# Turning finished tiles into columns by transposing transfers on SP's queue, in a two-layer transformer kernel

## Chip, cores and metric

The kernel runs on one core of one Trainium2 chip. The metric is the device time of one execution in microseconds; lower is better. The kernel before takes 1585.8 us (median of 3 runs).

## The reference

Four sequences of 512 tokens with 512 features go through two layers, each an attention part and a feed-forward part; after each of the four parts the residual is added and the sum is normalised over its 512 features (layer norm without weights). All weights are dense float32 except those of the first feed-forward part, which are int8 with a scale per column.

```
x = LN(x + lightning_attention(x))      # 16 heads of 32, rotated q and k, causal with decay, chunks of 128, then w_proj
x = LN(x + ((silu(x @ Wg * sg) * (x @ Wu * su)) @ Wd) * sd)                # 512 -> 2048 -> 512
x = LN(x + (x@Wq+bq) * cumsum((x@Wk+bk) * (x@Wv+bv), over tokens) * sigmoid(x@Wgt+bgt))
x = LN(x + mixture_of_experts(x))       # 32 experts of 192, top 8 of a softmax, the 5th to 8th choice rerouted by similarity
```

## The kernel before

Tokens are handled in NT = 16 tiles of P = 128, four tiles (TB) to a sequence. `X` holds the tiles by rows, one token per partition, in float32. A matrix product needs the tokens as columns, features on the partitions, so `XT` holds every tile a second time, transposed, as two float16 halves (a high half and the remainder) of four 128 x 128 blocks each. The kernel synchronises by hand: each engine has its own instruction stream, in the order of the code, and waits on semaphores.

A finished tile (number n, counted over all stages: 0 to 15 from attention, 16 to 31 from the feed-forward part, 32 to 47 from gated attention) gets into `XT` in these steps. VectorE (DVE) or ScalarE (ACT) writes the normalised tile to `X` and raises `x_new`. ACT copies it to float16, the high half of a small buffer (`hlA` in attention, the two places of `hlB` in the feed-forward part, the four places `hl4` in gated attention), and raises `x_hi`. GpSimd (POOL) subtracts to get the low half (`x_low`, line 1686) and raises `x_lo`. TensorE (PE) makes eight transposes of 128 x 128 float16 into one PSUM bank (`xt_transposes`, line 545), raising `xt_trans`, and ACT copies the bank to `XT` (`xt_copy`, line 1400), raising `xt_new` by one. All copies of ACT are put down to line 1395 in the profile.

Attention (0 to 318 us) is a loop over the 16 tiles. In step t, PE transposes q and k of tile t (line 602), makes the output projection of tile t-1 (line 652), the state update (line 636), scores (lines 616 and 617), the products with the state (line 627), the q and k projections of tile t+1 (line 562), the eight transposes of tile t-1 (line 551), the products with the chunk (line 644) and the v projection of tile t+1 (line 562). SyncE (SP) issues four transfers per step, `swap(t)` (line 394), that exchange the partition halves of q; they wait for the two copies out of PSUM (`evac_act`, `evac_dve`), and the scores wait for them. The transposes of tile 15 come in round 7 of the first feed-forward group.

The feed-forward part (318 to 666 us) has four groups of four tiles, each of 16 rounds m. A round is 8 gate matmuls (line 706), 8 up matmuls (line 712) and 8 down matmuls of the round before (line 735). ACT does silu of the gate (line 1508), the float16 half of the product, and a copy for weight preparation; DVE the rest. The gate matmuls of a round wait for the silu of the round before. The norms of the group before are made in rounds 0 to 4; in rounds 5 to 8 of groups 1 to 3 ACT fills `hlB` for one tile each, and PE transposes these in rounds 7 to 10. Beside this, in every round, the experts' weights are split into two halves for later: SP stores 640 KB to HBM (line 432) and loads the next 640 KB (line 428), four rounds ahead.

Gated attention (666 to 885 us) has four rounds q, one per sequence, each of four steps of 48 matmuls (line 562; `gate_proj`). ACT and POOL normalise and split the four tiles finished before; in round q these are tiles 28 to 31 for q = 0, then 32 to 35 and so on. PE transposes them in steps 1 and 2 (`norm_transposes`), and after step 2 of rounds 1 to 3 makes the router's `logits` for the sequence finished before from `XT` (line 562, 48 matmuls of 32 columns). The four tiles of the last sequence follow after the rounds. SP stores the halves by rows and `X` to HBM (`store_rows`, lines 497 and 498), waiting for `x_lo` of each tile.

After that come the routing tables (to 957 us), 159 blocks of experts (to 1541 us) and the last norm.

Of the kernel before, what the change touches and what calls it, by code (L numbers as in the profile page):

```python
# [24 lines left out]
P = 128  # L25
# [12 lines left out]
EPS = 1e-5  # L38
NBLK = TOK * TOPK // P + EXPERTS - 1
# [44 lines left out]
def build(nc, ins, out):  # L84
    ctx = ExitStack()
    with ctx:
# [287 lines left out]
        def _(sp):  # L374
# [24 lines left out]

            swap(0)  # L400
# [6 lines left out]
            load_piece(12)  # L407
            swap(2)
            load_piece(13)
            load_x(2)  # L410
            swap(3)
            load_piece(14)
            load_x(3)
            swap(4)
            load_piece(15)
            swap(5)
            swap(6)
# [5 lines left out]
            with sp.Fori(7, NT) as t:  # L423
                swap(t)
# [14 lines left out]
            prep_load(1, 2)  # L439
            sp.wait_ge(state_lo, NT + 1)  # L440
# [6 lines left out]
            for m in range(NM):  # L447
                sp.wait_ge(wp_lo, m + 1)
                prep_store(m // 2, m)
                prep_load((m + 4) // 2, m + 4)  # L450
                if m % 2 == 0 and m // 2 + 1 < len(wc_pieces):
                    sp.wait_ge(wc_lo, m // 2 + 1)
                    sp.dma_start(wcraw, wc_pieces[m // 2 + 1][0]).then_inc(wc_raw, 16)
            with sp.Fori(1, BATCH - 1) as g:
                for m in range(NM):
                    sp.wait_ge(wp_lo, g * NM + (m + 1))
                    prep_store(g * 8 + m // 2, m)
                    prep_load(g * 8 + (m + 4) // 2, m + 4)
            for m in range(NM):
                sp.wait_ge(wp_lo, (BATCH - 1) * NM + m + 1)  # L460
                prep_store((BATCH - 1) * 8 + m // 2, m)
                if m + 4 < NM:
                    prep_load((BATCH - 1) * 8 + (m + 4) // 2, m + 4)

# [38 lines left out]

            for b in range(BATCH - 2):
                store_rows(b)
                store_weights(b)
# [49 lines left out]
        def _(pe):  # L556
# [98 lines left out]
            def attention(t, first, last):  # L655
# [42 lines left out]
            def ffn(g, first):  # L698
                for m in range(NM):
                    s = g * NM + m  # L700
                    if m == 0:
                        pe.wait_ge(xt_new, g * TB + TB)
# [14 lines left out]
                    if first and m == 7:  # L717
                        xt_transposes(pe, NT - 1, NT - 1, hlA, bank[3])
# [49 lines left out]
            def norm_transposes(q, tt):  # L768
                n = 2 * NT - TB + q * TB + tt
                pe.wait_ge(xt_new, n)  # L770
                xt_transposes(pe, n, None, hl4[tt], bank[3])

            def logits(b):
# [5 lines left out]
                pe.wait_ge(xt_new, 2 * NT + (b + 1) * TB)  # L779
# [41 lines left out]
            for s in range(BATCH * KD):  # L821
                q, et = s // KD, s % KD
                if et == 0:
                    pe.wait_ge(xt_new, NT + (q + 1) * TB)
# [13 lines left out]
                if et == 2:  # L838
                    norm_transposes(q, 3)
# [3 lines left out]
                if et == 1:  # L843
                    norm_transposes(q, 0)
# [5 lines left out]
            for tt in range(TB):  # L850
                norm_transposes(BATCH, tt)
# [536 lines left out]
        def _(act):  # L1388
# [11 lines left out]
            def xt_copy(n, t, src):  # L1400
                act.wait_ge(xt_trans, n + 1)
# [51 lines left out]
            def attention(t, first, last):  # L1453
# [32 lines left out]
                if not first:  # L1486
                    xt_copy(t - 1, t - 1, bank[5])
# [15 lines left out]
            def ffn(g, first):  # L1503
                n0 = g * TB + (NT - TB)
                for m in range(NM):
# [14 lines left out]
                    if first and m == 1:  # L1520
                        act.wait_ge(x_new, NT)
                        act.wait_ge(xt_trans, NT - 1)
                        copy(hlA[:, 0, :], tile(NT - 1)).then_inc(x_hi, 1)
                    if first and m == 7:
                        xt_copy(NT - 1, NT - 1, bank[3])
# [6 lines left out]
                    if not first and 7 <= m < 7 + TB:  # L1532
                        xt_copy(n0 + (m - 7), n0 + (m - 7 - NT), bank[3])
# [7 lines left out]
            def high_half(q, tt):  # L1541
# [4 lines left out]
                act.wait_ge(xt_trans, 2 * NT - TB if q == 0 else n - TB + 1)  # L1546
# [22 lines left out]
            def norm_copy(q, tt):  # L1569
                n = 2 * NT - TB + q * TB + tt  # L1570
                xt_copy(n, n % NT, bank[3])
# [14 lines left out]
            for s in range(BATCH * KD):  # L1586
                q, et = s // KD, s % KD
                if et == 2:
                    norm_copy(q, 0)
# [13 lines left out]
                if et == 2:  # L1603
                    norm_copy(q, 1)
                    if q >= 2:
                        row_hots(q - 2, 0, 8)
                    norm_copy(q, 2)
# [3 lines left out]
                if et == 2:  # L1611
                    norm_copy(q, 3)
# [10 lines left out]
            for tt in range(TB):  # L1623
                norm_copy(BATCH, tt)
# [308 lines left out]
```

## Time and profile before

| | |
|---|---|
| median of 3 runs | 1585.8 us (1585.67 to 1586.67) |
| profiled execution | 1585.89 us, span 1584.0 us |
| PE busy | 1448.3 us (91% of the span) |
| DVE, ACT, POOL busy | 952.9, 732.3, 776.5 us |
| mean granted TensorE clock | 0.961 of full speed |
| transfers issued from SP | 183.08 MB, 35.0% of 16 DMA engines over the span |

The profile is taken from one execution; its span runs from the first to the last instruction, and the execution's own time is 1.9 us longer. Busy times of engines overlap. The profile also shows the chain of work that ended last, followed back from the last instruction to what released each step.

### The profile page before, as it was taken

To read this page: it belongs to the slowest core of one execution; us is meant where nothing else is said; L and a number is where in the kernel's file an instruction comes from. 1 tells how busy PE (TensorE), PEld (TensorE's weight loads), DVE (VectorE), ACT (ScalarE), POOL (GpSimd) and SP (SyncE) were. 2 spreads that over 40 slices of the span, in tenths; PEclk is the share of its full clock that TensorE was granted. 3 is DMA by queue.
4 is the path that set the end of the run, shared out by engine and by line. 5 is a ranking of instruction groups with operands and counts; after the bars stand their busy time and mean duration, and the time that the engine had idled before them with its cause. 6 is when DMAs were issued, how large, how long until landed. Compare 5 with 4: busy or idle time off the path is not lost.

```text
span 1584.0 us, 33491 instructions
## 1 busy us (share of the span) xinstructions
PE 1448.3 (91%) x11191; PEld 820.2 (52%) x11192; DVE 952.9 (60%) x1858; ACT 732.3 (46%) x1326; POOL 776.5 (49%) x691
## 2 busy tenths in 40 slices
PE   5999999999999999999998358999999999999990
PEld 2566666544444444445454215666666666666650
DVE  7877777776757666634988883444444444444435
ACT  6544433555464645444446442444444444444443
POOL 3565544530010202044445536777777777777655
PEclk9999999999999999999999668999999999999995
DMA  6323111269776868531101444888989898876767
GB/s 242 107 81 107 27 40 26 77 219 315 238 255 232 265 222 268 179 139 54 55 3 54 158 165 93 185 183 166 202 177 206 177 196 186 162 108 96 177 76 230
DMA packets 102991, 243.45 MB, mean 154 GB/s; under 512 B 21481, under 2 KB 23049, under 8 KB 101904
## 3 DMA queue, kind: packets, MB, share of 16 engines
q1 hardware_dynamic: 67312, 183.08, 35.0%
q0 software_dynamic: 35616, 59.58, 23.0%
q8 instruction: 34, 0.56, 0.1%
q14 instruction: 29, 0.24, 0.0%
HBM read 158.92 MB, written 101.71 MB: 165 GB/s over the span
## 4 chain that ended last, share of the span: by engine, by line
PE 68%; DVE 16%; issue 6%; POOL 4%; ACT 3%; DMA 2%; SPq 0%; DVEq 0%; POOLq 0%; ACTq 0%
PE bank L894 20%; PE bank L915 11%; PE bank L562 8%; PE bank L706 6%; PE bank L712 6%; PE bank L735 6%; PE bank L885 5%; PE bank L904 2%; ACT ARENA L1395 1%; POOL ARENA L1695 1%; DVE ARENA L1032 1%; POOL ARENA L1690 1%; DVE ARENA L1266 1%; DVE ARENA L985 1%; PE bank L551 1%
## 5 line engine op out<-in xcount | busy, mean ns | idle before, releaser
L894 PE MATMUL bank<-ARENA,XT 128*128 x1908 | 364.2, 327 | 2.2 <-issue 1.1
L1826 POOL DMA_INDIRECT accs<-X,WA x159 | 252.5, 1588 | 98.8 <-issue 34.7
L894 PEld LDWEIGHTS bank<-ARENA,XT 128*128 128x128 f16 x1908 | 180.4, 98 | 124.2 <-issue 8.2
L1356 DVE COPY XT<-bank 128x1024 f16<-128x1024 f16 x159 | 109.9, 691 | 182.3 <-PE bank L885 181.1
L1819 POOL DMA_INDIRECT XT<-x_rows,WA x159 | 166.5, 1047 | 87.0 <-issue 39.8
L1395 ACT ACTIVATE ARENA<-ARENA 128x512 f16<-128x512 f32 (+2 forms) x128 | 89.3, 709 | 245.5 <-DVE ARENA L1114 134.1
L915 PE MATMUL bank<-ARENA,XT 128*128 x795 | 197.4, 379 | 0.9 <-issue 0.9
L1649 ACT ACTIVATE XT<-bank 128x192 f32<-128x192 f32 x159 | 52.5, 330 | 287.7 <-PE bank L894 287.7
L562 PE MATMUL bank<-XT,STG 128*128 128x512 f16 x640 | 151.8, 385 | 4.6 <-DVE ARENA L1160 4.3
L1677 POOL TENSOR_TENSOR rstd<-mv,mhalf 128x1 f32<-128x1 f32 x28 | 8.7, 309 | 258.2 <-DVE mv L964 258.2
L1395 ACT ACTIVATE XT<-bank 128x384 f16<-128x384 f16 (+2 forms) x207 | 125.7, 607 | 9.5 <-PE bank L551 9.0
L562 PE MATMUL bank<-WA,XT 128*128 128x512 f16 (+1 forms) x732 | 127.1, 327 | 2.4 <-DVE ARENA L1013 1.6
L735 PE MATMUL bank<-ARENA 128*128 128x512 f16 x512 | 121.0, 379 | 3.5 <-DVE ARENA L1120 3.4
L706 PE MATMUL bank<-XT,WA 128*128 (+1 forms) x512 | 122.6, 383 | 1.0 <-issue 1.0
L1366 DVE SCALAR_TENSOR_TENSOR XT<-bank,XT 128x192 f32<-128x192 f32 x159 | 66.4, 418 | 95.0 <-ACT XT L1649 91.8
L712 PE MATMUL bank<-XT,ARENA 128*128 (+1 forms) x512 | 121.7, 381 | 0.0
L1686 POOL TENSOR_TENSOR ARENA<-X,ARENA 128x512 f16<-128x512 f32 (+1 forms) x48 | 66.6, 1401 | 88.5 <-ACT ARENA L1395 88.5
L885 PE MATMUL bank<-ident,XT 128*128 128x128 f16 x1272 | 97.8, 220 | 5.5 <-DMA XT<-x_rows,WA 5.5
L915 PEld LDWEIGHTS bank<-ARENA,XT 128*128 128x128 f16 x795 | 71.7, 98 | 57.3 <-issue 1.4
L562 PEld LDWEIGHTS bank<-XT,STG 128*128 128x128 f16 x640 | 62.1, 99 | 74.8 <-DVE ARENA L1160 5.6
L885 PEld LDWEIGHTS bank<-ident,XT 128*128 128x128 f16 x1272 | 85.0, 98 | 25.7 <-issue 6.0
L1395 ACT ACTIVATE X<-bank 128x512 f32<-128x512 f32 x159 | 93.1, 586 | 2.1 <-PE bank L915 2.1
(245 smaller groups left out, 2369.6 us busy)
## 6 DMA issues: line engine op xcount, KB each, us to landing
w_scratch<-WA SPq DMA_DIRECT2D x64, 640.0 KB, 3.9
ARENA<-w_scratch SPq DMA_DIRECT2D x64, 640.0 KB
ARENA<-w_exp SPq DMA_DIRECT2D x48, 640.0 KB, 5.2
WA<-w_exp SPq DMA_DIRECT2D x16, 640.0 KB, 5.1
ARENA<-ARENA SPq DMA_DIRECT2D x64, 128.0 KB, 2.3
accs<-ARENA SPq DMA_DIRECT2D x20, 256.0 KB, 3.1
X<-x SPq DMA_DIRECT2D x4, 1024.0 KB, 6.6
ARENA<-wc SPq DMA_DIRECT2D x8, 512.0 KB, 6.0
```

The source lines that it names most:

```text
L562: mm = pe.matmul(dst, wa(a, k), wb(b, k), start=n == 0, stop=n == 3 * KD - 1)
L706: mm = pe.matmul(bank[0][:, :], Wg[:, n % KD, m * P:(m + 1) * P], XT[:, n // KD, n % KD, tk], start=n == 0, stop=n == 2 * KD - 1)
L712: mm = pe.matmul(bank[1 + m % 2][:, :], Wu[:, n % KD, m * P:(m + 1) * P], XT[:, n // KD, n % KD, tk], start=n == 0, stop=n == 2 * KD - 1)
L735: mm = pe.matmul(bank[4 + tt][:, :], fB[:, m % 2, a, tt * P:(tt + 1) * P], Wd[:, m, :], start=m == 0 and a == 0, stop=m == NM - 1 and a == 1)
L885: mm = pe.transpose(d[:, c * P:(c + 1) * P], xg[k.u % NG].bitcast(F16)[:, c * P:(c + 1) * P], ident16[:, :])
L894: mm = pe.matmul(d, xTb[k.u % 2][:, a * KD + kd, :], weights(sl, b, kd * 2 * DFF, 2 * DFF), start=(a, b, kd) == (0, 0, 0), stop=(a, b, kd) ...
L915: mm = pe.matmul(d, hT[k.u % 2][:, c, :], weights(sl, j, c0, DIM), start=n == 0, stop=n == 4)
L1356: dve.tensor_copy(xTb[k.u % 2].rearrange("p c n -> p (c n)"), bank[k.u % 2][:, :].bitcast(F16)).then_inc(xt_sb, 1)
L1395: return act.activation(dst, src, ACT.Copy, scale=scale)
L1686: pool.tensor_tensor(hl[:, 1, :], tile(t), hl[:, 0, :], ALU.subtract).then_inc(x_lo, 1)
L1819: pool.indirect_dma_start(xg[i % NG], None, xrows, bass.IndirectOffsetOnAxis(blkidx[:, i:i + 1], 0), bounds_check=TOK - 1, oob_is_err=Fals ...
L1826: pool.indirect_dma_start(accs, bass.IndirectOffsetOnAxis(blkout[:, i:i + 1], 0), yD[i % 8], None, compute_op=ALU.add).then_inc(y_out[i % ...
```

## The change

The 44 tiles 0 to 43 get into `XT` by one transposing transfer each, SBUF to SBUF, that SP issues. PE's transposes and ACT's copies of these tiles are gone; tiles 44 to 47, the last sequence, keep them. `xt_new` now rises by 16 with each landed transfer, and all waits on it are scaled; `MOVED` is 3 * 16 - 4 = 44.

```diff
+MOVED = 3 * NT - TB
...
+            def xt_move(n, t, hl):
+                sp.wait_ge(x_lo, n + 1)
+                if isinstance(n, int):
+                    sp.wait_ge(xt_new, n * 16)
+                sp.dma_start_transpose(XT[:, :, :, bass.ds(t * P, P)].rearrange("p a k n -> p (a k) n"),
+                                       hl.rearrange("p a n -> p (a n)")).then_inc(xt_new, 16)
```

SP's order. In attention the transfer of tile t-2 stands ahead of `swap(t)`; that of tile 14 behind the first loads of expert weights; that of tile 15 in round 3 of the first feed-forward group. In groups 1 to 3 they stand in rounds 5 to 8, behind the round's store and load. In gated attention the four of a round stand ahead of `store_rows`.

```diff
             with sp.Fori(7, NT) as t:
+                xt_move(t - 2, t - 2, hlA)
                 swap(t)
...
             prep_load(1, 2)
+            xt_move(NT - 2, NT - 2, hlA)
             sp.wait_ge(state_lo, NT + 1)
...
+                if m == 3:
+                    xt_move(NT - 1, NT - 1, hlA)
             with sp.Fori(1, BATCH - 1) as g:
                 for m in range(NM):
                     sp.wait_ge(wp_lo, g * NM + (m + 1))
                     prep_store(g * 8 + m // 2, m)
                     prep_load(g * 8 + (m + 4) // 2, m + 4)
+                    if 5 <= m < 5 + TB:
+                        xt_move(g * TB + (NT - TB + m - 5), g * TB + (m - 5 - TB), hlB[:, m % 2])
...
             def store_rows(b):
+                if b < BATCH - 1:
+                    for tt in range(TB):
+                        xt_move(2 * NT + b * TB + tt, b * TB + tt, hl4[tt])
...
+            for tt in range(TB):
+                xt_move(2 * NT - TB + tt, NT - TB + tt, hl4[tt])
             for b in range(BATCH - 2):
                 store_rows(b)
```

PE, in attention, the feed-forward part and gated attention:

```diff
-                if not first:
-                    pe.wait_ge(s_decayed, t * 4 + 4)
-                    xt_transposes(pe, t - 1, t - 1, hlA, bank[5])
...
-                        pe.wait_ge(xt_new, g * TB + TB)
+                        pe.wait_ge(xt_new, g * (16 * TB) + 16 * TB)
...
-                    if first and m == 7:
-                        xt_transposes(pe, NT - 1, NT - 1, hlA, bank[3])
...
-                    if not first and 7 <= m < 7 + TB:
-                        n = g * TB + (NT - TB + m - 7)
-                        pe.wait_ge(xt_new, n)
-                        xt_transposes(pe, n, None, hlB[:, m % 2], bank[3])
...
-                pe.wait_ge(xt_new, 2 * NT + (b + 1) * TB)
+                pe.wait_ge(xt_new, 16 * (2 * NT + (b + 1) * TB) if b < BATCH - 1 else 16 * MOVED + TB)
...
-                if et == 2:
-                    norm_transposes(q, 1)
...
-                if et == 2:
-                    norm_transposes(q, 2)
...
-                if et == 2:
-                    norm_transposes(q, 3)
...
-                if et == 1:
-                    norm_transposes(q, 0)
```

ACT loses `xt_copy` at the same places, and its writes to the small buffers wait for landed transfers. In the feed-forward part the wait is now for the transfers of all tiles before; it was for the transposes of the tile two back:

```diff
                 if not first:
                     act.wait_ge(x_new, t)
+                    act.wait_ge(xt_new, (t - 1) * 16)
                     copy(hlA[:, 0, :], tile(t - 1)).then_inc(x_hi, 1)
...
                         act.wait_ge(x_new, n0 + tt + 1)
-                        if tt >= 2:
-                            act.wait_ge(xt_trans, n0 + tt - 1)
+                        act.wait_ge(xt_new, g * (16 * TB) + 16 * (NT - TB + tt))
                         copy(hlB[:, m % 2, 0, :], tile(n0 + (tt - NT))).then_inc(x_hi, 1)
...
-                act.wait_ge(xt_trans, 2 * NT - TB if q == 0 else n - TB + 1)
+                act.wait_ge(xt_new, 16 * (2 * NT - TB if q == 0 else n - TB + 1))
```

## Rows read from the trace of the kernel before

**Rows 1.** The page, chain that ended last: share of the span by engine.

```profile
PE 68%; DVE 16%; issue 6%; POOL 4%; ACT 3%; DMA 2%; SPq 0%; DVEq 0%; POOLq 0%; ACTq 0%
```

**Rows 2.** Windows by stage: us, busy us (count) per engine, PEclk, DMA share, GB/s.

```profile
0.00:318.00 318.00, 288.22 (x3692) 180.72 (x3693) 244.58 (x358) 150.78 (x186) 161.99 (x114) 0.99 0.29 89
318.00:666.00 348.00, 343.79 (x1649) 156.43 (x1650) 233.20 (x282) 183.60 (x229) 44.55 (x43) 0.99 0.74 246
666.00:885.00 219.00, 199.70 (x1218) 103.34 (x1216) 151.12 (x352) 103.87 (x182) 102.47 (x144) 0.97 0.18 65
```

**Rows 3.** Timeline of PE in one attention step: start us, duration us, instruction, [idle before].

```profile
227.70 0.61 PE L551 MATMUL bank<-ident,ARENA 128*128 128x128 f16 x8
228.24 1.08 PE L644 MATMUL bank<-ARENA 128*32 128x128 f32 x32
...
236.33 1.12 PE L636 MATMUL bank<-ARENA 128*64 128x32 f32 x32
237.73 0.23 PE L616 MATMUL bank<-ARENA 128*128 128x128 f16 x1 [0.28 <-DMA ARENA<-ARENA]
```

**Rows 4.** Timeline of POOL and SP's queue in the same step.

```profile
223.42 1.16 POOL L1686 TENSOR_TENSOR ARENA<-X,ARENA 128x512 f16<-128x512 f16 x1 [2.54 <-ACT ARENA L1395]
...
232.44 2.35 POOL L1695 TENSOR_TENSOR ARENA<-ARENA,small 128x1024 f32<-128x1024 f32 x1
...
233.59 2.39 SPq L398 DMA_DIRECT2D ARENA<-ARENA  x4
```

**Rows 5.** Timeline of PE in the feed-forward part, rounds 7 to 9 of group 1.

```profile
448.68 0.61 PE L551 MATMUL bank<-ident,ARENA 128*128 128x128 f16 x8
449.13 1.89 PE L706 MATMUL bank<-XT,WA 128*128 x8
...
454.76 1.89 PE L706 MATMUL bank<-XT,WA 128*128 x8
```

**Rows 6.** Timeline of PE in gated attention: the logits, and a wait in round 2.

```profile
745.37 1.35 PE L562 MATMUL bank<-WA,XT 128*128 128x32 f16 x48
...
787.33 4.02 PE L562 MATMUL bank<-XT,STG 128*128 128x512 f16 x10 [2.15 <-DVE ARENA L1160]
...
798.13 1.35 PE L562 MATMUL bank<-WA,XT 128*128 128x32 f16 x48
...
852.06 1.35 PE L562 MATMUL bank<-WA,XT 128*128 128x32 f16 x48
```

**Rows 7.** DMA issues: tensors, queue, count, KB each, median us to landing.

```profile
ARENA<-w_exp SPq DMA_DIRECT2D x48, 640.0 KB, 5.2
...
x_rows<-ARENA SPq DMA_DIRECT2D x16, 256.0 KB, 2.5
...
XT<-x_rows,WA POOLq DMA_INDIRECT x159, 4.3
...
WA<-sim SPq DMA_DIRECT2D x4, 4.0 KB, 1.7
```

**Rows 8.** DMA queues, 770 to 772 us (one store, 128-byte rows): packets, MB, share.

```profile
q1 hardware_dynamic: 515, 0.06, 19.6%
```

**Rows 9.** Timeline of ACT, POOL and SP's queue, feed-forward rounds 5 and 6.

```profile
445.34 0.61 ACT L1395 ACTIVATE ARENA<-X 128x512 f16 x1
445.86 0.67 ACT L1508 ACTIVATE ARENA<-bank,small 128x512 f32<-128x512 f32 x1
...
442.14 1.83 POOL L1686 TENSOR_TENSOR ARENA<-X,ARENA 128x512 f16<-128x512 f16 x1 [7.25 <-ACT ARENA L1395]
...
443.86 0.47 SPq L428 DMA_DIRECT2D ARENA<-w_exp  x1
```

**Rows 10.** Timeline of SP's queue in gated attention: first row store of each round.

```profile
729.63 0.32 SPq L497 DMA_DIRECT2D x_rows<-ARENA  x1
...
781.38 0.32 SPq L497 DMA_DIRECT2D x_rows<-ARENA  x1
...
837.00 0.32 SPq L497 DMA_DIRECT2D x_rows<-ARENA  x1
```

More of the change, by code:

```diff
@@ L407, in _ @@
             load_piece(12)
+            xt_move(0, 0, hlA)
             swap(2)
@@ L410, in _ @@
             load_x(2)
+            xt_move(1, 1, hlA)
             swap(3)
@@ L413, in _ @@
             load_x(3)
+            xt_move(2, 2, hlA)
             swap(4)
             load_piece(15)
+            xt_move(3, 3, hlA)
             swap(5)
+            xt_move(4, 4, hlA)
             swap(6)
@@ L463, in _ @@
                     prep_load((BATCH - 1) * 8 + (m + 4) // 2, m + 4)
+                if 5 <= m < 5 + TB:
+                    xt_move(2 * NT - 2 * TB + m - 5, NT - 2 * TB + m - 5, hlB[:, m % 2])
             def load_expert(e):
@@ L766, in back, with norm_transposes @@
                 mm.then_inc(at_ready, 1)
[L768 to L771, printed above, removed]
+            def norm_transposes(tt):
+                pe.wait_ge(xt_new, 16 * MOVED + tt)
+                xt_transposes(pe, MOVED + tt, None, hl4[tt], bank[3])
             def logits(b):
@@ L823, in _ @@
                 if et == 0:
-                    pe.wait_ge(xt_new, NT + (q + 1) * TB)
+                    pe.wait_ge(xt_new, 16 * (NT + (q + 1) * TB))
                 gate_proj(s, 0)
@@ L850, in _ @@
             for tt in range(TB):
-                norm_transposes(BATCH, tt)
+                norm_transposes(tt)
             ranks(2)
@@ L1400, in xt_copy @@
             def xt_copy(n, t, src):
-                act.wait_ge(xt_trans, n + 1)
+                act.wait_ge(xt_trans, n - MOVED + 1)
                 copy(XT[:, :, :, bass.ds(t * P, P)].rearrange("p a k n -> p (a k) n"),
@@ L1485, in attention @@
                 copy(oH.rearrange("p a b -> p (a b)"), oT.rearrange("p a b -> p (a b)")).then_inc(o_hi, 1)
-                if not first:
-                    xt_copy(t - 1, t - 1, bank[5])
             def convert(k):
@@ L1521, in ffn @@
                         act.wait_ge(x_new, NT)
-                        act.wait_ge(xt_trans, NT - 1)
+                        act.wait_ge(xt_new, 16 * (NT - 1))
                         copy(hlA[:, 0, :], tile(NT - 1)).then_inc(x_hi, 1)
-                    if first and m == 7:
-                        xt_copy(NT - 1, NT - 1, bank[3])
                     if not first and 5 <= m < 5 + TB:
@@ L1528, in ffn @@
                         act.wait_ge(x_new, n0 + tt + 1)
-                        if tt >= 2:
-                            act.wait_ge(xt_trans, n0 + tt - 1)
+                        act.wait_ge(xt_new, g * (16 * TB) + 16 * (NT - TB + tt))
                         copy(hlB[:, m % 2, 0, :], tile(n0 + (tt - NT))).then_inc(x_hi, 1)
-                    if not first and 7 <= m < 7 + TB:
-                        xt_copy(n0 + (m - 7), n0 + (m - 7 - NT), bank[3])
             ffn(0, True)
@@ L1567, in row_hots, with norm_copy @@
                         act.activation(oneR[b][i % ring], away[(m - 1) % 2], ACT.Relu, scale=-1.0, bias=1.0).then_inc(row_act, 1)
-            def norm_copy(q, tt):
-                n = 2 * NT - TB + q * TB + tt
-                xt_copy(n, n % NT, bank[3])
+            def norm_copy(tt):
+                xt_copy(MOVED + tt, NT - TB + tt, bank[3])
             def exponentials(b):
@@ L1587, in _ @@
                 q, et = s // KD, s % KD
-                if et == 2:
-                    norm_copy(q, 0)
                 act.wait_ge(kc_ready, s + 1)
@@ L1603, in _ @@
                 if et == 2:
-                    norm_copy(q, 1)
                     if q >= 2:
                         row_hots(q - 2, 0, 8)
-                    norm_copy(q, 2)
                 act.wait_ge(qc_ready, s + 1)
@@ L1610, in _ @@
                 act.activation(qC, bank[2][:, :], ACT.Identity, scale=1 / WS, bias=biasC[:, et:et + 1]).then_inc(qc_sb, 1)
-                if et == 2:
-                    norm_copy(q, 3)
                 if et == 3 and q >= 2:
@@ L1623, in _ @@
             for tt in range(TB):
-                norm_copy(BATCH, tt)
+                norm_copy(tt)
             exponentials(3)
```

## The prediction, made before the change was built

> **What bounds the kernel now.** I read the page first: TensorE (PE) holds 68% of the chain that ended last [rows 1]. A share of the whole span of 1584.0 us says nothing about one stage, so next came the windows by stage. In the attention stage (0 to 318 us) PE is busy for 288.2 us, in the feed-forward stage (318 to 666 us) for 343.8 of 348 [rows 2]. DMA differs most: its engines are busy 29% of the time in the first and 74% in the second [rows 2]. In the third, gated attention (666 to 885 us), PE is busy for 199.7 of 219 us and DMA for 18%. The experts, after it, hold no step of the change. Last came the timelines around one tile's transposes in each stage, to see what releases them, what they delay, and what a transfer in their place would have to beat.
>
> The profiled execution took 1585.89 us for its span of 1584.0; the median of the runs is 1585.8. I sum against 1585.9. Within 0.2% (3.2 us) is about what a measurement of this kernel can tell from no change.
>
> **What goes: TensorE's share.** Of the 48 tiles, 44 lose their eight transposes and one ScalarE (ACT) copy. In attention there are 15, for tiles 0 to 14. PE starts them at 227.70 and the next matmuls at 228.24, so one tile costs 0.54 us [rows 3]. PE is the binding loop there, busy for 288 of 318 us [rows 2], and the copy that ACT loses ran beside PE's next group; I cost its removal at nothing, and if PE's cover were gone it would be one copy per tile more to gain. Will the 0.54 us reach the end of the step? The L636 group that follows at 236.33 needs a GpSimd (POOL) result that ends at 232.44 + 2.35 = 234.79; 1.54 us are left, enough [rows 3, 4]. The scores wait 0.28 us for the swap transfers, but those start at 233.59, after the value projection and the first transposes of the step, so they move forward with PE [rows 3, 4]. So attention gives 15 x 0.54 = 8.1 us. In a feed-forward round the transposes cost 449.13 - 448.68 = 0.45 us [rows 5]: 0.4 us for the one in the first group, 1.8 us in each of three later groups of four. In gated attention I take the same 0.45 us per tile: 1.8 us in round 0 and in round 1; in rounds 2 and 3 PE stands for 2.15 us on VectorE (DVE) soon after the first two tiles, which swallows these, so 0.9 each [rows 6]. That is 5.4 us. If nothing waited for the transfers, the gain would be 8.1 + 0.4 + 5.4 + 5.4 = 19.3 us.
>
> **What is added: 44 transfers on SP's queue.** The trace has no transposing transfer, so its time from issue to landing, L below, must be bounded. From below: a 256 KB copy out of the same kind of tile lands after 2.5 us [rows 7]. From above: if the 16 source rows that lie side by side give runs of 16 x 2 = 32 bytes, a 256 KB tile is 8192 pieces. One row shows what small pieces cost: 515 packets of mostly 128 bytes kept 16 engines 19.6% busy in 2 us, 0.196 x 16 x 2 / 515 = 12.2 ns of engine time each [rows 8]. 8192 x 12.2 / 16 = 6.2 us, and with the 1.7 us that a 4 KB transfer takes from issue to landing [rows 7] an estimate of 7.9 us. The nearest row in shape is the gather by rows, 4.3 us [rows 7], and that moves pieces of 2176 bytes, so a transposition should not be cheaper. I take the middle of the bounds, 5.2 us, and keep both ends.
>
> The Trainium skill holds two rules that point opposite ways. "VectorE: DVE Perf Modes", The three transpose paths, gives 1309 ns for a 128 x 128 block by the DMA crossbar against 390 ns on TensorE and advises TensorE where PSUM will do; eight blocks in series would be 10.5 us by that page, and the sum below would come to some 140 us lost. "Advanced Engine Details and Errata", X-Bar Transpose (TRN2), says that such transfers run as fast as regular ones; then L is near the lower bound and the change gains. No row here shows either.
>
> **Attention, transfers.** The move of a tile is issued when POOL's low half is done, 223.42 + 1.16 = 224.58 in this step; SP's next duty is the swap at 233.59 [rows 4]. So 9.0 us are free for SP and its queue, and ACT overwrites the tile's source only a step later. At L = 5.2 the cost is nothing; beyond 9 us each further us would delay 14 swaps, and the scores behind them.
>
> **Feed-forward, transfers.** Here the wait is new. ACT may fill the double buffer for tile tt only when the moves of all earlier tiles have landed; before, it waited for the transposes of the tile two back. In round 5 POOL's half is ready at 442.14 + 1.83 = 443.97, but SP issues a 640 KB load at 443.86, which needs 5.2 us [rows 7, 9]. The move queues behind it and lands near 450.0. ACT's copy for the next tile ran at 445.34 and is pushed by 4.7 us; so is the silu behind it, which ended at 446.53 and now ends at 451.2 [rows 9]. PE's gate matmuls of round 8, due at 449.13 - 0.45 = 448.7, wait for it: 2.5 us lost [rows 5]. Two rounds' gate matmuls start 454.76 - 449.13 = 5.63 us apart, 5.2 without the transposes [rows 5]. The two rounds after repeat the loop copy 0.6, hand-over 0.2, POOL 1.83, issue 0.1, move L: 2.7 + L = 7.9 us against these 5.2 us, a further 2.7 us each. One group loses 2.5 + 5.4 - 1.8 = 6.1 us; three lose 18.3 us. Behind the waiting ACT instruction stands the silu, behind that all of PE; behind SP's wait stand a weight store and a load, which were issued four rounds ahead and have room.
>
> **Gated attention, transfers.** Each move waits for the landing of the one before, so four take 4 x (L + 0.1) = 21.2 us. In round 1 the first half is ready at 729.6 (SP stored its rows at 729.63), so the last lands at 750.8; the logits ran at 745.37 and would, 1.8 us earlier, want them at 743.6: 7.2 us lost [rows 6, 10]. Round 2: 781.4 + 21.2 = 802.6 against 798.13 - 0.9 = 797.2, 5.4 us lost; round 3: 837.0 + 21.2 = 858.2 against 851.2, 7.0 us [rows 6, 10]. Round 0's moves are needed only in round 3. Lost 19.6, gained 5.4: 14.2 us net. The row stores behind the moves on SP are pushed by as much; what comes next on SP waits for the router's weights anyway, which come after the logits.
>
> **Sum.** -8.1 - 0.4 + 18.3 + 14.2 = +24.0: **1610 us**. L enters twice in each of three groups and four times in each of three rounds, so between 3.8 and 9 us the sum is 18 L - 69.6: zero at 3.9 us.
>
> **Rivals.** (1) *The transfer is an ordinary one*, L = 2.5. The gated moves take 10.4 us and all land in time; the feed-forward groups lose 2.5 us each for the move behind the load and gain 1.8; the sum is -8.1 - 0.4 + 2.1 - 5.4 = -11.8, 1574 us. For it: the same bytes in the copy [rows 7] and queues that stand idle in two of the three stages [rows 2]. Against it: the copy moves whole rows; and if the swap wait of 0.28 us [rows 3] grows by what PE saves, attention gives nothing and 1582 us remain. It decides from L = 3.7 downward. This is what the Trainium skill's page on advanced details would have. (2) *The transfer is far dearer*, 10 us and more: the formula gives +110, and attention's swaps come late by 1 us in 14 steps, about 1710 us. Small pieces speak for it [rows 8]; at two bytes a piece, 131072 pieces, one transfer would take 100 us and the kernel milliseconds. Against it: the 29% DMA load in attention leaves the engines free [rows 2]. The Trainium skill's page on VectorE, taken block by block, falls here. (3) *A draw*: L between 3.7 and 4.1, where waits and savings cancel to within 3.2 us, about 1586 us. The gather's 4.3 us lies just above it [rows 7].
>
> **Chances.** Forecast (L from 4.1 to 9) 0.40; far dearer 0.16; ordinary transfer 0.35; draw 0.09. So faster 0.35, same 0.09, slower 0.56. The two slower cases belong together, and their range begins at 1590. For 8 in 10 the range reaches down over the ordinary transfer, to 1570 (the feed-forward load not in its way takes off 5 more), and up to 1690, where L is near 9.5; about 0.03 lie below and 0.13 above.
>
> **What would show it.** The issue-to-landing time of the new transfers is the first thing to read: 5.2 us by the forecast, 2.5 by the first rival. Right: no L551 matmuls but those of the last four tiles (32), attention steps 0.5 us shorter, ACT idle before its copy into the feed-forward buffer with the transfer as releaser, PE waiting for silu three times a group, and PE idle before the logits of rounds 1 to 3 by 5 to 7 us. Wrong: logits at their old distance, or feed-forward groups no longer than before. If attention steps do not get shorter, the step on the swaps has failed; if they get longer, the 9 us of room are too few. PE's granted clock falling to its lower level after new waits would add to every loss; I have set nothing for it.

## The result: 1592.2 us, 0.4% slower; 1610 us had been predicted

| | before | after |
|---|---|---|
| median | 1585.67 us (9 runs, 1583.53 to 1587.54) | 1592.18 us (9 runs, 1586.09 to 1597.38) |
| ratio after / before | | 1.0039, 95% interval 1.0026 to 1.0052 |
| profiled execution | 1585.89 us, span 1584.0 us | 1586.09 us, span 1584.2 us |

The change costs 6.2 us by the ratio (0.0039 x 1585.7). The direction is as forecast and the time lies in the range; the size is a quarter of the 24 us forecast. One caution for all that follows: the profiled execution of after is the lowest of its nine runs, so its trace shows the waits but not the whole loss.

The page and the windows by stage of after (columns as in [rows 1, 2]):

```profile
PE 60%; DVE 17%; issue 8%; DMA 5%; POOL 4%; ACT 4%; SPq 1%; ACTq 0%; DVEq 0%; POOLq 0%
```

```profile
0.00:318.00 318.00, 284.71 (x3585) 174.96 (x3587) 246.56 (x361) 139.19 (x174) 165.33 (x115) 0.98 0.36 103
318.00:666.00 348.00, 332.24 (x1512) 146.91 (x1511) 226.92 (x276) 167.62 (x211) 35.07 (x42) 0.99 0.77 253
666.00:885.00 219.00, 198.01 (x1113) 98.66 (x1110) 154.13 (x354) 90.82 (x169) 102.18 (x144) 0.97 0.31 87
```

DMA has gone from 2% to 5% of the chain, and PE is busy for 11.6 us less in the feed-forward window (343.79 to 332.24), though only 13 tiles' transposes are gone there, 13 x 0.45 = 5.9 us: the rest is waiting. First the price of a transfer, from the view of the line that issues it: L is again the time from issue to landing. The first two lines are over the span, the pairs after them over attention (from 50 us), the feed-forward part and gated attention:

```profile
L405 SPq DMA_TRANSPOSE XT<-ARENA x44: 1232/1240/1906, 58.5 to 848.2; - x44
DMA to landing us min/median/max: 3.0/3.1/5.9
...
L405 SPq DMA_TRANSPOSE XT<-ARENA x15: 1232/1240/1361, 58.5 to 312.2; - x15
DMA to landing us min/median/max: 3.0/3.0/4.6
...
L405 SPq DMA_TRANSPOSE XT<-ARENA x13: 1257/1513/1906, 343.8 to 639.4; - x13
DMA to landing us min/median/max: 3.1/5.4/5.9
...
L405 SPq DMA_TRANSPOSE XT<-ARENA x16: 1232/1232/1533, 697.8 to 848.2; - x16
DMA to landing us min/median/max: 3.0/3.0/4.2
```

L is 3.0 us where SP's queue is empty, and 5.4 us in the median of the feed-forward part. So the 5.2 us taken for it hold in one stage only. SP itself is held for 1.24 us by each in the median, 1.51 in the feed-forward part.

Attention in after, the PE and SP timelines of the step of [rows 3, 4]:

```profile
232.45 1.12 PE L662 MATMUL bank<-ARENA 128*64 128x32 f32 x32
233.84 0.23 PE L642 MATMUL bank<-ARENA 128*128 128x128 f16 x1 [0.27 <-DMA ARENA<-ARENA]
```

```profile
211.99 2.39 SPq L399 DMA_DIRECT2D ARENA<-ARENA  x4
221.34 1.24 SPq L405 DMA_TRANSPOSE XT<-ARENA  x1
229.72 2.38 SPq L399 DMA_DIRECT2D ARENA<-ARENA  x4
```

The swaps are 17.73 us apart (229.72 - 211.99), and the move is out of SP's way 7.1 us before the next swap (221.34 + 1.24 to 229.72). The scores wait 0.27 us as before.

The feed-forward part, rounds 5 to 8 of group 1: ACT's copies into `hlB`, PE's gate matmuls, and SP's queue. This answers to [rows 5, 9].

```profile
444.08 0.63 ACT L1403 ACTIVATE ARENA<-X 128x512 f16 x1 [4.81 <-DMA XT<-ARENA]
449.47 0.63 ACT L1403 ACTIVATE ARENA<-X 128x512 f16 x1 [1.49 <-DMA XT<-ARENA]
457.44 0.63 ACT L1403 ACTIVATE ARENA<-X 128x512 f16 x1 [4.08 <-DMA XT<-ARENA]
```

```profile
445.35 2.50 PE L729 MATMUL bank<-XT,WA 128*128 x8 [2.66 <-ACT ARENA L1515]
447.64 3.02 PE L735 MATMUL bank<-XT,ARENA 128*128 x8
...
458.69 1.90 PE L729 MATMUL bank<-XT,WA 128*128 x8 [1.13 <-ACT ARENA L1515]
```

```profile
437.69 0.47 SPq L442 DMA_DIRECT2D ARENA<-w_exp  x1
438.41 1.74 SPq L405 DMA_TRANSPOSE XT<-ARENA  x1
440.97 0.57 SPq L446 DMA_DIRECT2D w_scratch<-WA  x1
441.74 0.46 SPq L442 DMA_DIRECT2D ARENA<-w_exp  x1
446.20 1.83 SPq L405 DMA_TRANSPOSE XT<-ARENA  x1
449.72 0.57 SPq L446 DMA_DIRECT2D w_scratch<-WA  x1
450.49 0.45 SPq L442 DMA_DIRECT2D ARENA<-w_exp  x1
451.58 1.53 SPq L405 DMA_TRANSPOSE XT<-ARENA  x1
```

The first move is issued 0.7 us behind a load at 437.69 and the copy it releases starts at 444.08, 5.7 us later; the second has no load just ahead of it and takes 3.3 us (446.20 to 449.47); the third is behind a load again, 5.9 us (451.58 to 457.44). PE waits 2.66 us at the first. Its gate and up matmuls after that wait take 2.50 and 3.02 us instead of the 1.9 that eight take otherwise: the mean granted clock from 445.3 to 450 us is 0.64, part of it at the lower level of 1.2 GHz, where the stretches around it have 1.00. By their starts that is another 1.7 us. Over the three groups ACT waits nine times, 30.6 us in all, and PE six times for the silu behind it, 12.8 us in all. The last down matmuls of the stage start 5.5 us late, before and after:

```profile
664.91 1.90 PE L735 MATMUL bank<-ARENA 128*128 128x512 f16 x8 [0.51 <-DVE ARENA L1120]
...
670.39 1.90 PE L752 MATMUL bank<-ARENA 128*128 128x512 f16 x8 [0.51 <-DVE ARENA L1128]
```

Gated attention, [rows 6, 10]. PE, then SP's moves of rounds 1 and 2:

```profile
747.27 1.35 PE L588 MATMUL bank<-WA,XT 128*128 128x32 f16 x48
...
789.21 4.45 PE L588 MATMUL bank<-XT,STG 128*128 128x512 f16 x10 [3.51 <-DVE ARENA L1168]
...
800.11 1.35 PE L588 MATMUL bank<-WA,XT 128*128 128x32 f16 x48
...
854.71 1.35 PE L588 MATMUL bank<-WA,XT 128*128 128x32 f16 x48
```

```profile
733.32 11.58 SPq L405 DMA_TRANSPOSE XT<-ARENA  x4
...
783.27 10.54 SPq L405 DMA_TRANSPOSE XT<-ARENA  x4
```

In round 2 four serial moves take 10.54 us from the first issue until SP is done with the last, (10.54 - 1.24) / 3 = 3.1 us each; in round 1 it is 11.58. No logits wait, but in round 1 it is close: the last move lands at about 733.32 + 11.58 - 1.24 + 3.0 = 746.7 us (an estimate from these rows), the logits start at 747.27. The stage began 5.5 us late; its logits are 1.9, 2.0 and 2.7 us late (747.27, 800.11 and 854.71 against 745.37, 798.13 and 852.06 of [rows 6]), and the first group behind them that waits for POOL, before and after, 0.2 us:

```profile
877.24 0.66 PE L765 MATMUL bank<-ident,ARENA 128*128 128x128 f32 x4 [2.40 <-POOL ARENA L1777]
...
877.41 0.66 PE L782 MATMUL bank<-ident,ARENA 128*128 128x128 f32 x4 [2.40 <-POOL ARENA L1772]
```

### The profile page after: what moved, and what is told of

Same layout as the page of the kernel before. It is cut to its first block, busy times and chain, and to the rows that moved or that the text cites. A ratio compares the mean times of both kernels' runs of the same rounds, so it can differ in the third digit from the quotient of the medians.

```text
span 1584.2 us, 32802 instructions
## 1 busy us (share of the span) xinstructions
PE 1431.7 (90%) x10839; PEld 800.8 (51%) x10840; DVE 952.3 (60%) x1858; ACT 692.1 (44%) x1282; POOL 769.3 (49%) x691
## 2 busy tenths in 40 slices
DMA packets 149453, 254.96 MB, mean 161 GB/s; under 512 B 67945, under 2 KB 69513, under 8 KB 148368
## 4 chain that ended last, share of the span: by engine, by line
PE 60%; DVE 17%; issue 8%; DMA 5%; POOL 4%; ACT 4%; SPq 1%; ACTq 0%; DVEq 0%; POOLq 0%
PE bank L902 20%; PE bank L923 11%; PE bank L588 8%; PE bank L893 5%; PE bank L729 4%; PE bank L735 4%; PE bank L752 3%; DMA XT<-ARENA 3%; ACT WA L1403 2%; PE bank L912 2%; DVE bs L969 2%; ACT ARENA L1403 1%; POOL ARENA L1685 1%; DVE ARENA L1274 1%; POOL ARENA L1690 1%
## 5 line engine op out<-in xcount | busy, mean ns | idle before, releaser
L729 PE MATMUL bank<-XT,WA 128*128 (+1 forms) x512 | 123.1, 384 | 15.2 <-ACT ARENA L1515 12.8
L1681 POOL TENSOR_TENSOR ARENA<-X,ARENA 128x512 f16<-128x512 f32 (+1 forms) x48 | 60.5, 1273 | 119.6 <-ACT ARENA L1403 119.6
L729 PEld LDWEIGHTS bank<-XT,WA 128*128 128x128 f16 x512 | 49.8, 99 | 78.4 <-ACT ARENA L1515 16.1
```

The costliest lines, as they stand in the source:

```text
L729: mm = pe.matmul(bank[0][:, :], Wg[:, n % KD, m * P:(m + 1) * P], XT[:, n // KD, n % KD, tk], start=n == 0, stop=n == 2 * KD - 1)
```

## The experiments

The kernel before, timed beside them on the same chip, had a median of 1586.0 us for the three kernels of one stage and the one with four places, 1586.3 for the next four (feed-forward on PE, the move ahead, four places with the move between, the ordinary copy), and 1586.4 for the last two.

### One stage at a time

Each of three kernels keeps the transfers of one stage and gives the other tiles back to PE and ACT, in the places of the kernel before. The core of the edit after which only attention goes by transfer:

```diff
-                    if 5 <= m < 5 + TB:
-                        xt_move(g * TB + (NT - TB + m - 5), g * TB + (m - 5 - TB), hlB[:, m % 2])
...
+                    if not first and 7 <= m < 7 + TB:
+                        n = g * TB + (NT - TB + m - 7)
+                        pe.wait_ge(xt_new, g * (16 * TB) + 16 * (NT - TB + m - 7))
+                        xt_transposes(pe, n, None, hlB[:, m % 2], bank[3])
...
-                if b < BATCH - 1:
-                    for tt in range(TB):
-                        xt_move(2 * NT + b * TB + tt, b * TB + tt, hl4[tt])
```

The other two are its mirror: `xt_move` goes in two stages, `xt_transposes` and `xt_copy` come back there.

> Theory (the losses sit in the feed-forward groups, where ScalarE waits for a transfer that stands behind a weight load; attention is a plain gain): only the 16 tiles of attention go by transfer, the other 28 as before. The step shortens from 18.17 to 17.73 us as in the changed kernel, 14 to 15 times, so 6 to 7 us less than before: about 1579.5 us. Rival (transposing transfers cost something everywhere, by contention or by the serial queue, and the profile of one run hides it): no gain here, 1583 us or more.

Attention alone: 1581.72 us, ratio 0.9975 (0.9967 to 0.9984): a gain, but of 4.3 us where 6 to 7 were expected.

> Theory: only the 12 tiles of feed-forward groups 1 to 3 go by transfer. The two stalls of TensorE per group (2.7 and 1.1 to 2.6 us in the changed kernel's trace) and the matmuls at the lower clock behind them outweigh the 1.8 us of transposes saved: 3 x 3.9 = 11.7 us lost at the end of the stage, of which the stages behind may take back up to 2: 1595 to 1598 us, and more spread between runs than before, because the clock falls behind some stalls and not behind others. Rival: the loss belongs to the combination (attention ends earlier and shifts the pieces), then this one is within 3 us of before.

Feed-forward alone: 1598.89 us, ratio 1.0082 (1.0069 to 1.0095), 0.9 us above what was expected; its five runs lie within 2.5 us, no wider than those of before. ACT waits nine times for transfers, 31.0 us in all, as in after. PE's timeline has the last down matmuls of the stage 10.5 us late (675.42 against 664.91):

```profile
675.42 1.90 PE L749 MATMUL bank<-ARENA 128*128 128x512 f16 x8 [0.51 <-DVE ARENA L1138]
```

> Theory: only the 16 tiles of gated attention go by transfer. All land before the logits want them (3.1 us each, four in a row 12.4 us against 14), TensorE saves 3.6 us up to round 1, and VectorE's routing work, which bounds rounds 2 and 3, takes the rest: between 0 and 4 us less than before, 1582 to 1586 us. Rival: the four transfers in a row hold up the logits or the row stores: 1588 us or more.

Gated attention alone: 1581.54 us, ratio 0.9973 (0.9963 to 0.9983), 0.5 us below the range that was expected.

So the parts are -4.3, +12.9 and -4.5 us, +4.1 together, near the 6.2 measured. The loss is all in the feed-forward part; the other two stages gain.

> Attention and gated stages by transfer, the twelve FFN tiles by TensorE transposes and ScalarE copies as before. Theory A (the loss lies in the FFN stage and the stages add): attention alone gave -4.3 us, the gated stage alone -4.5 us, so this gives 1586.0 - 8.8 = 1577 us (1575 to 1580), FFN ends near 657 us of the span. Theory B (the transfers of one stage start the next one in a worse position, or the saving is shared because both end in the same rounds of the gated stage): about 1581.5 us, no better than either alone.

Measured: 1577.66 us, ratio 0.9957 (0.9941 to 0.9972). The two gaining stages add: 1577.7 us against the 1577.2 of their sum, with an interval of 2.5 us to each side. Against after, the feed-forward transfers alone cost 14.5 us by the medians (1592.2 - 1577.7), 13.0 by the two ratios.

### The feed-forward part: the queue, and the two places

First the move goes to the head of SP's round, ahead of the wait, the store and the load (the last group is changed alike):

```diff
                 for m in range(NM):
+                    if 5 <= m < 5 + TB:
+                        xt_move(g * TB + (NT - TB + m - 5), g * TB + (m - 5 - TB), hlB[:, m % 2])
                     sp.wait_ge(wp_lo, g * NM + (m + 1))
                     prep_store(g * 8 + m // 2, m)
                     prep_load(g * 8 + (m + 4) // 2, m + 4)
-                    if 5 <= m < 5 + TB:
-                        xt_move(g * TB + (NT - TB + m - 5), g * TB + (m - 5 - TB), hlB[:, m % 2])
```

> All three stages by transfer, as in the changed kernel, but in rounds 5 to 8 of each FFN group SyncE issues the move ahead of the round's weight store and 640 KB load instead of behind them. Theory A (the queue costs it): in the changed kernel the first and third moves of a group land 5.6 and 5.8 us after they are issued, against 3.2 us for the second, which has no load ahead of it; ahead of the load all four should land after 3.1 to 3.3 us, so the first wait of the ScalarE copy falls from 4.81 us to about 2.3 and TensorE's gap of 2.66 us in a group goes. The last FFN matmul ends at 659 to 664 us of the span instead of 670.4, and the time is 1576 to 1582 us. Theory B (the two places cost it, whatever the queue does): a place is free only when its transfer has landed, each of the rounds 7 to 10 still waits, the FFN ends at 667 us or later and the time stays at 1587 to 1592 us. A gap of about 2 us with a late load in its place (the load is now issued behind a wait for the low half) would be a third case: waits of VectorE or GpSimd for weight pieces appear.

Measured: 1580.47 us, ratio 0.9960 (0.9947 to 0.9973). ACT and SP's moves in group 1:

```profile
444.11 0.63 ACT L1409 ACTIVATE ARENA<-X 128x512 f16 x1 [1.87 <-DMA XT<-ARENA]
449.83 0.63 ACT L1409 ACTIVATE ARENA<-X 128x512 f16 x1 [1.82 <-DMA XT<-ARENA]
455.65 0.63 ACT L1409 ACTIVATE ARENA<-X 128x512 f16 x1 [1.84 <-DMA XT<-ARENA]
```

```profile
440.91 1.27 SPq L411 DMA_TRANSPOSE XT<-ARENA  x1
442.44 0.57 SPq L452 DMA_DIRECT2D w_scratch<-WA  x1
443.19 0.47 SPq L448 DMA_DIRECT2D ARENA<-w_exp  x1
446.23 1.27 SPq L411 DMA_TRANSPOSE XT<-ARENA  x1
```

The same 44 transfers and the same bytes, twelve of them ahead of their round's store and load: 3.2 us from issue to the copy that it releases (440.91 to 444.11), waits of 1.9 us instead of up to 4.8, and 11.7 us less than after (1592.2 - 1580.5). ACT's wait to use a place again is still there, nine times, 15.6 us in all, and leaves PE waits of at most 0.5 us in this group; the last down matmuls of the stage start at 658.40 us.

Next the halves get four places instead of two, in `hl4`, idle in this stage, and the queue order is again that of the change. ACT's part of the edit (POOL's half and SP's move take the same buffer):

```diff
-                        act.wait_ge(xt_new, g * (16 * TB) + 16 * (NT - TB + tt))
-                        copy(hlB[:, m % 2, 0, :], tile(n0 + (tt - NT))).then_inc(x_hi, 1)
+                        if tt == 0:
+                            act.wait_ge(wc_lo, len(wc_pieces))
+                            act.wait_ge(xt_new, g * (16 * TB) + 16 * (NT - TB))
+                        copy(hl4[tt][:, 0, :], tile(n0 + (tt - NT))).then_inc(x_hi, 1)
```

> The changed kernel with four places for the feed-forward halves instead of two (the two others lie in a buffer that is free by then), so that ScalarE waits once per group for transfers of the group before. Theory: the stalls of TensorE in rounds 8 and 10 go, and the 1.8 us per group stay as a gain; against the changed kernel 3 x (3.9 + 1.8) = 17 us less, about 1574 us (1570 to 1578). Rival (the transfers themselves slow the weight loads or TensorE by contention): most of the loss stays, 1585 us or more.

Measured: 1574.26 us, ratio 0.9925 (0.9912 to 0.9938), the lowest of all. ACT's copies have no wait for a transfer left:

```profile
437.81 0.61 ACT L1409 ACTIVATE ARENA<-X 128x512 f16 x1
...
451.29 0.61 ACT L1409 ACTIVATE ARENA<-X 128x512 f16 x1
```

The transfers still land late, after 5.9 us in the median of this stage; nobody waits. The last down matmuls start at 656.03 us. Beside the kernel that keeps these twelve tiles on PE (1577.7 us) the feed-forward transfers now gain 3.4 us instead of costing 14.5.

The next kernel puts the move between the round's store and load in this one:

```diff
                     prep_store(g * 8 + m // 2, m)
+                    if 5 <= m < 5 + TB:
+                        xt_move(g * TB + (NT - TB + m - 5), g * TB + (m - 5 - TB), hl4[m - 5])
                     prep_load(g * 8 + (m + 4) // 2, m + 4)
-                    if 5 <= m < 5 + TB:
-                        xt_move(g * TB + (NT - TB + m - 5), g * TB + (m - 5 - TB), hl4[m - 5])
```

> The FFN stage with four places for the halves (as in the earlier run with four places, 1574.3 us), and the move issued between the round's store and its load. Theory A (with four places no landing is waited for in rounds 7 to 10, the queue no longer matters): 1573 to 1576 us, FFN end near 656 us as in that run. Theory B (there is still a wait behind the load at the first copy or at the next group's first up-projection): 1569 to 1572 us.

Measured: 1575.11 us, ratio 0.9932 (0.9918 to 0.9946), no different from the four places with the order of the change (the intervals overlap). Once no landing is waited for, no cost of the order is left to measure. Its moves, with the 640 KB store just ahead of them and the load behind, land after 6.2 us in the median of this stage: a load just ahead is not needed for a late landing.

> Attention by transfer, the FFN stage by transfer with four places, the gated stage by TensorE. Theory A (the gated stage's gain of 4.5 us adds to the rest): 1574.3 + 4.5 = 1579 us (1577 to 1581). Theory B (most of that gain is lost once the FFN stage ends early): 1574 to 1576 us.

Its edit is the four places above, with gated attention's tiles back on PE. Measured: 1580.11 us, ratio 0.9966 (0.9952 to 0.9979), 5.9 us over the kernel with four places. The gated stage gives its gain here too. Against attention alone (1581.7 us) the feed-forward transfers with four places take off 1.6 us, in intervals that overlap.

### What turning costs

An ordinary transfer of the same bytes takes the place of each transposing one. This kernel leaves the tiles unturned, so all that follows works on wrong values:

```diff
-                sp.dma_start_transpose(XT[:, :, :, bass.ds(t * P, P)].rearrange("p a k n -> p (a k) n"),
-                                       hl.rearrange("p a n -> p (a n)")).then_inc(xt_new, 16)
+                sp.dma_start(XT[:, :, :, bass.ds(t * P, P)].rearrange("p a k n -> p (a k) n"),
+                             hl.rearrange("p a (k n) -> p (a k) n", n=P)).then_inc(xt_new, 16)
```

> The changed kernel with each transposing transfer replaced by an ordinary transfer of the same 256 KB between the same places, issued at the same points of the same queue: the columns are not turned, so the values of the layers behind are wrong rows. It measures what turning costs. Theory A (a queue and its bytes set the landing, not the turning): an ordinary transfer lands after about 2.7 to 3.1 us as the transposing one does, about 5 to 6 us behind a load, and the time stays near 1592 us (1588 to 1595). Theory B (turning costs): the ordinary one lands after 2.5 us or less in the attention stage and issues in far less than the 1.24 us that SyncE takes for a transposing one; the FFN's first wait falls below 4 us and the time is 1582 to 1588 us.

Measured: 1591.02 us, ratio 1.0033 (1.0017 to 1.0048), as after. Its transfers by the same view:

```profile
L405 SPq DMA_DIRECT2D XT<-ARENA x44: 614/654/920, 59.0 to 855.1; - x44
DMA to landing us min/median/max: 2.9/2.9/7.1
```

Turning costs 0.1 us of landing at the minimum (3.0 against 2.9) and 0.6 us more of SP's time to issue (1.24 against 0.65). In the feed-forward part the ordinary transfer lands late too, after 5.7 us in the median. Both kernels have some 46,000 more packets than before, nearly all under 512 bytes; for the transposing one:

```profile
DMA packets 149453, 254.96 MB, mean 161 GB/s; under 512 B 67945, under 2 KB 69513, under 8 KB 148368
```

Before, it was 102,991 in all. (149453 - 102991) / 44 = 1056 more packets per tile (1040 for the ordinary copy), near the 1024 that 256 KB make in pieces of 256 bytes, one row of 128 tokens in `XT`. The prediction's small-piece bound had 8192. What a packet costs can be read from the share of SP's queue, before and after:

```profile
q1 hardware_dynamic: 67312, 183.08, 35.0%
...
q1 hardware_dynamic: 113776, 194.62, 38.7%
```

That is 0.037 x 16 x 1584 us for 46,464 packets, some 20 ns of engine time each, an estimate that lays the whole rise on the new packets.

### The room in gated attention

From the kernel with gated attention alone by transfer, each of twelve moves made twice in series:

```diff
+            def xt_twice(t, hl):
+                sp.wait_ge(x_lo, 2 * NT + t + 1)
+                sp.wait_ge(xt_new, (2 * NT + t) * 16)
+                sp.dma_start_transpose(XT[:, :, :, t * P:(t + 1) * P].rearrange("p a k n -> p (a k) n"),
+                                       hl.rearrange("p a n -> p (a n)")).then_inc(out_done, 16)
+                sp.wait_ge(out_done, 16 * (t + 1))
...
                     for tt in range(TB):
+                        xt_twice(b * TB + tt, hl4[tt])
                         xt_move(2 * NT + b * TB + tt, b * TB + tt, hl4[tt])
...
-            sp.wait_ge(out_done, 16 * NT)
+            sp.wait_ge(out_done, 16 * (NT + 12))
```

> The gated stage alone by transfer (that kernel took 1581.5 us), with each of the twelve moves of its first three groups made twice in series, so that eight transfers of 3.1 to 3.2 us take the place of four: some 25 us from the first issue to the last landing, where the prediction had put 21.2 us for four. Theory A (the prediction's way was right and only its duration was off: four moves have 14 to 16 us of room before the logits that read them): the logits of the three groups wait for the transfers, 11.6, 9.8 and 11.4 us by the prediction's own working, less what TensorE already loses to VectorE in these rounds (3.5 us in two of them); the time is 1600 to 1615 us and the trace shows three waits of 7 to 12 us for the transfer. Theory B (the logits are not held, since what waits for the transfer is not on TensorE's path, and the room is much larger than 16 us): under 1590 us, waits below 3 us.

Measured: 1611.12 us, ratio 1.0157 (1.0143 to 1.0171). The three logits in PE's timeline:

```profile
751.53 1.44 PE L589 MATMUL bank<-WA,XT 128*128 128x32 f16 x48 [10.62 <-DMA XT<-ARENA]
...
814.13 1.44 PE L589 MATMUL bank<-WA,XT 128*128 128x32 f16 x48 [8.13 <-DMA XT<-ARENA]
...
877.83 1.44 PE L589 MATMUL bank<-WA,XT 128*128 128x32 f16 x48 [9.03 <-DMA XT<-ARENA]
```

Waits of 10.6, 8.1 and 9.0 us where 11.6, 9.8 and 11.4 were expected, less what PE loses to DVE in two of the rounds; 27.8 together, and 29.6 us on the time (1611.1 - 1581.5) for twelve more moves. The prediction's room for four moves was 14.0, 15.8 and 14.2 us (743.6 - 729.6, 797.2 - 781.4, 851.2 - 837.0): 12.4 us (4 x 3.1) fit, 25 do not.

## Why the prediction was right in direction and off in size

**Attention, -8.1 us forecast, -4.3 measured.** The step shrank by 0.44 us (18.17 to 17.73), not the 0.54 of PE's own time, and only 13 steps shrank, not 15: PE's third state update is not earlier (72.74 us before, 73.00 after), its last is 5.7 us earlier (309.02, 303.35). After it PE waits longer, 2.43 us instead of 1.00 ahead of the first gate matmuls, which start at 315.35 instead of 318.72. But in the trace of before these gate matmuls and the up matmuls behind them ran for 3.57 and 2.59 us with a mean granted clock of 0.50 from 318 to 322 us, the lower level, against 1.89 each at 1.00 in that of after, so that nothing is lost at the seam in these two traces: at the last down matmuls of the first group PE is 6.2 us ahead (399.92 against 406.09), which includes the 0.45 us of tile 15. With attention alone by transfer the last down matmuls of the feed-forward part start 5.1 us earlier (659.83 against 664.91). Forecast right: swaps move forward with PE, the 0.27-us wait stays, the transfers are hidden. What remains between these numbers and the total of 4.3 us was not traced further.

**Feed-forward, +17.9 us forecast with the first group's -0.4 (18.3 - 0.4), +12.9 alone and 13.0 to 14.5 inside the change.** The mechanism is as forecast: move behind the load, ACT's copy held, the silu behind it, PE's gate matmuls: 2.66 us where 2.5 stood. The first move behind its load has the size forecast. The two moves after it were summed with L = 5.2 each and 1.83 us for POOL's half, a loop of 7.9 us. In fact POOL's half takes 1.15 us there and the second move 3.3, a loop of 5.4 us (444.08 to 449.47) with PE not held; the third takes 5.9 us because a load stands before it again, a loop of 8.0 (449.47 to 457.44), of which 1.13 us reach PE. So PE's waits in the three groups are 12.8 us, where 23.7 (3 x 7.9) stood in the sum; the matmuls at the lower clock behind some of them come on top, for which the sum had nothing. Run with the move ahead of the store and load, 11.7 us of this loss go. Four places show that it is the reuse of `hlB` that turns a late landing into a stall.

**Gated attention, +14.2 us forecast, -4.5 measured. This is the step that failed**, and by itself it is as large as the whole error. The term "four take 4 x (L + 0.1) = 21.2 us" was mis-sized: they take 12.4. The three lost pieces of 7.2, 5.4 and 7.0 us vanish. The 5.4 us of saved transposes come out in size (the stage takes 5.3 us less in the trace of after), but not where they were put: 3.6 us are gained up to the first logits, as forecast; PE's waits for DVE in rounds 2 and 3 rise from 2.15 to 3.5 us, and by the last logits 0.8 us are lost again instead of 1.8 gained; 2.5 us come back behind the logits, which the sum did not have. That part of the agreement is luck. Doubling the moves brought the loss back as the working says; so the room was right, the price wrong. The price came from the middle between 2.5 and 7.9 us, a bound that supposed pieces of 32 bytes. The main fault is the count of the pieces, and the length of the destination's rows, 256 bytes, would have given nearly the right one. With 1056 packets the same working gives 1056 x 12.2 / 16 + 1.7 = 2.5 us; with the 20 ns estimated above for a packet it gives 3.0, which is what was measured.

With L = 3.1 in the prediction's own working, the gated stage gives -5.4, the feed-forward part +5.7 (2.5 + 2 x 0.6 - 1.8 per group) and the sum is -8.2 us: faster. The measured +6.2 differs from that by 14.4 us: 7.6 to 9.2 in the feed-forward part (+5.3 with the first group against 12.9 to 14.5), 3.8 in attention, 0.9 in the gated stage, and up to 2 that the noise can hold. So one price for all 44 transfers was the deeper fault: L is 3.0 us on an empty queue and 5.4 us in the median where 640 KB loads and stores share it. With 5.2 us kept in the feed-forward part and 3.1 elsewhere the working gives -8.1 - 0.4 + 18.3 - 5.4 = +4.4 us. That this lies near 6.2 is in part luck too, since attention gained 3.8 us less and the feed-forward part cost some 4 us less than it has them. The direction rests on the feed-forward part alone.

**The rivals.** The ordinary transfer (1574 us, L = 2.5) was near the landing of an idle queue and wrong about the time: it let only the first move of a group cost anything. That four places reach 1574.3 us is another way to the same number. The Trainium skill's "Advanced Engine Details and Errata", X-Bar Transpose (TRN2), has transposing transfers as fast as regular ones: 3.0 against 2.9 us here, this case agrees. The Trainium skill's "VectorE: DVE Perf Modes", The three transpose paths, has 1309 ns for one block; eight in one transfer take 3.0 us here, not the 10.5 estimated from it. The far dearer transfer falls. The draw's condition, one L between 3.7 and 4.1, is met nowhere, though its 1586 us lie nearer to the measured time than the forecast's 1610.

**Open.** The profile of after shows a span only 0.2 us above before, while the median is 6.2 us above. The mean granted clock of its nine runs goes from 0.953 to 0.958, the profiled one at 0.958; the longest run (1597.4 us) has 0.954, and before has 0.960 to 0.963. The traces show where some of it goes: in after the lower clock follows PE's first wait in two of the three feed-forward groups (mean 0.64 and 0.65 over the next 4.5 us) and not in the third, and in the ordinary copy's trace, of a run of 1595.1 us, a wait in each of the three groups. Whether that makes up the whole difference between the runs is not shown, and what decides between one wait and the next was not tried; the prediction had set nothing for it. Nor is it shown whether the queue itself or the engines busy with the load and store delay a move issued close behind them: a move on another engine's queue was not tried.

## What to carry to other kernels

Price a transfer by its place in its queue, not by its size alone: read what is issued on that queue in the microsecond before it, and put a transfer that another engine waits for ahead of bulk loads that nobody needs yet. Before taking a wait for granted, count the places of the buffer; two more places were worth 18 us here (1592.2 to 1574.3) and needed no faster transfer. When an unknown duration enters a sum many times, work out the time at which the answer turns, as was done (3.9 us), and then look for the room of each stage apart, because one value for all stages hides that they turn at different points.

## What was not expected of the hardware

- A 256 KB transposing transfer from 128 x 1024 float16 to eight 128 x 128 blocks takes 3.0 us, 0.1 us more than an ordinary one between the same places. It makes about 1056 packets, 248 bytes each on average.
- It holds the issuing SyncE for 1.24 us, against 0.65 us for the ordinary one, and up to 1.9 us in the feed-forward part, where the DMA share is 0.77.
- Issued 0.7 us behind a 640 KB load on the same queue, it releases the copy that waits for it after 5.7 us; with a 640 KB store just ahead and the load behind, the median landing is 6.2 us; ahead of both, the copy is released after 3.2 us.
